# First expert layer's results stored in slot order and gathered by token in the attention stage, in a two-layer block on one Trainium2 core

## The reference

```python
# layer 0, experts: 8 experts, hidden size 512, two per token
h = layernorm(x) * (1 + cb) + sb
top_w, top_idx = top_k(softmax(h @ router_w.T), 2); top_w /= top_w.sum() + 1e-9
y = relu(h @ w1[e].T + b1[e]) @ w2[e].T + b2[e]          # for the token's two experts e
x = x + gb * (top_w[0] * y[0] + top_w[1] * y[1])
# layer 1, mixer ("attention")
h = layernorm(x) * (1 + ca) + sa
xn = h * rms_weight / sqrt(mean(h * h) + eps)
s  = gated_scan(sigmoid(xn @ w_A + b_A), (xn @ w_x) * sigmoid(xn @ w_output))
x  = x + ga * ((sigmoid(xn @ w_sidegate) * s) @ w_o + h)
# layer 1, experts: 16 experts, hidden size 256, two per token
```

## Time and profile before

| | us |
|---|---|
| time, median of 3 runs (lowest to highest) | 678.8 (677.65 to 682.81) |
| span of the profiled execution | 729.4 |
| time of the profiled execution around the span | not recorded |
| first to last tile of the first expert layer in the profile (first `up0` to last scatter) | 320.6 to 445.4 |
| attention, up to the first sigmoid, in the profile | 446.8 to 481.4 |

### The profile page before, as it was taken

One profiled execution on the slowest core, in us unless ns is written; L12 is line 12 of the kernel. 1 busy time (PEld: TensorE's weight loads), 2 busy tenths in 40 slices (PEclk: granted clock), 3 DMA queues, 4 the chain that ended last, 5 costly groups with the idle time before them and its releaser, 6 DMA issues.

```text
span 729.4 us, 9280 instructions
## 1 busy us (share of the span) xinstructions
PE 547.5 (75%) x2190; PEld 331.5 (45%) x2191; DVE 476.8 (65%) x847; ACT 340.9 (47%) x680; POOL 423.8 (58%) x324
## 2 busy tenths in 40 slices
PE   7599779989977889676676695669977677567730
PEld 3234224334423334555576683237545565446620
DVE  5867989997899898822532243646913777745427
ACT  3747445654755443412212235655615778950005
POOL 2576869998986897055555654500065771277650
PEclk8869969989997799978989998989968999796765
DMA  5432424332232330135556675000111121311115
GB/s 179 133 102 80 154 78 168 109 115 102 103 116 69 119 96 20 34 105 154 179 146 182 171 231 144 1 1 1 58 40 36 44 41 14 126 40 43 43 56 154
DMA packets 45438, 69.06 MB, mean 95 GB/s; under 512 B 6162, under 2 KB 25460, under 8 KB 45268
## 3 DMA queue, kind: packets, MB, share of 16 engines
q1 hardware_dynamic: 39828, 57.17, 25.1%
q0 software_dynamic: 5568, 11.41, 5.9%
HBM read 59.45 MB, written 9.11 MB: 94 GB/s over the span
## 4 chain that ended last, share of the span: by engine, by line
PE 53%; DVE 13%; issue 13%; ACT 9%; DMA 4%; another core or an unknown queue 3%; DVEq 2%; POOL 2%; SPq 1%; ACTq 1%; POOLq 0%
PE ps L1180 12%; PE ps L1325 6%; PE ps L1336 5%; PE ps L1143 4%; PE ps L1521 4%; DVE hs L1820 4%; PE ps L1174 4%; PE ps L1376 2%; PE ps L1485 2%; PE ps L1510 2%; PE ps L1087 1%; DVEq L1886 1%; DVE prod L1830 1%; ACT ps L709 1%
## 5 line engine op out<-in xcount | busy, mean ns | idle before, releaser
L521 POOL TENSOR_TENSOR bu<-uT,b_sb 128x1024 f32<-128x1024 f32 x62 | 145.0, 2356 | 1.6 <-DVE uT L1792 1.4
L475 POOL DMA_INDIRECT y_dram<-ys,rows_i x87 | 91.1, 1048 | 91.0 <-DVE ys L2078 38.2
L1180 PE MATMUL ps<-prod,cst 128*128 128x512 f32 x256 | 130.6, 655 | 3.2 <-DVE yT L1840 3.2
L469 POOL DMA_INDIRECT xl<-h_dram,rows_i x87 | 90.3, 1038 | 68.5 <-DVE rows_i L1704 36.1
L709 ACT ACTIVATE ps<-dtT,neg_a 128x512 f32<-128x512 f32 x128 | 85.5, 686 | 64.7 <-DVE hs L1820 63.6
L532 POOL TENSOR_TENSOR prod<-hs,c_sb 128x1024 f32<-128x1024 f32 x32 | 75.6, 2363 | 38.4 <-DVE hs L1820 21.4
L1180 PEld LDWEIGHTS ps<-prod,cst 128*128 128x128 f32 x256 | 50.4, 207 | 82.4 <-issue 77.1
L1820 DVE TENSOR_TENSOR_SCAN hs<-ps,carry,bu 128x512 f32<-128x512 f32 x64 | 77.6, 1264 | 4.5 <-ACT ps L709 4.5
L1820 DVE TENSOR_TENSOR_SCAN hs<-ps,bu 128x512 f32<-128x512 f32 x64 | 74.0, 1206 | 7.4 <-ACT ps L709 7.2
L1336 PE MATMUL ps<-w_s,ht 128*128 x312 | 47.5, 300 | 32.8 <-issue 19.4
L842 ACT ACTIVATE ht<-ps,b1T 128x128 f32<-128x128 f32 x78 | 24.7, 366 | 86.0 <-PE ps L1325 56.4
(11 more groups left out here) (293 smaller groups left out, 950.1 us busy)
## 6 DMA issues: line engine op xcount, KB each, us to landing
b_sb<-b_rows SPq DMA_DIRECT2D x31, 512.0 KB
w1r<-in_w SPq DMA_DIRECT2D x39, 256.0 KB
c_sb<-b_rows SPq DMA_DIRECT2D x32, 256.0 KB, 3.6
mf_s<-in_mf SPq DMA_DIRECT2D x16, 256.0 KB
w_s<-in_w SPq DMA_DIRECT2D x9, 256.0 KB, 4.0
h_dram<-h_tok SPq DMA_DIRECT2D x8, 256.0 KB
phase_s<-in_phase SPq DMA_DIRECT2D x16, 128.0 KB
down_s<-in_down SPq DMA_DIRECT2D x1, 2048.0 KB, 7.4
```

Source lines behind the costliest of these rows:

```text
L469: pool.indirect_dma_start(xl[:, j % slots, :], None, h_dram[l], bass.IndirectOffsetOnAxis(ap=rows_i[:, 0, j:j + 1], axis=0)).then_inc(load ...
L475: pool.indirect_dma_start(y_dram[l], bass.IndirectOffsetOnAxis(ap=rows_i[:, 1, j:j + 1], axis=0), ys[:, j % XR, :], None).then_inc(saved[j ...
L521: nc.gpsimd.tensor_tensor(bu[:, g % RING, :, :], uT[:, c % 2, :, :], b_sb[:, k % BRING, g % 2, :].unsqueeze(1).broadcast_to([P, ND, CHUNK] ...
L1180: last = nc.tensor.matmul(bank(Y_BANK + d), ident, prod[:, g % RING, d, :], start=n == 0, stop=n == NS - 1)
```

## The change

The first layer's results are stored as they come. `y_dram[0]` now has one row for each slot (39 * 128), and SP stores tile j of `ys0` to rows j * 128 and up with a plain DMA (`store_tile`), five tiles behind its weight loads; the second layer's weights stay where they were among the loads. `bias_down` waits for these stores in place of the scatters. POOL only gathers inputs during the layer, up to 16 tiles ahead. When all stores have landed, POOL gathers the results by token: for each of the 16 token tiles and both picks one indirect DMA that reads 128 rows of `y_dram[0]` by the slot numbers (`slot_i`, which VectorE copies out of `slot_f`), 32 in all, in the order of the chunks. SP's 8 loads are gone. What POOL did in the attention's entry moves: the weighting to ScalarE (4 instructions a chunk), the inverse deviation to ScalarE (`rstd`, two small instructions a chunk) and VectorE (`minus_mean`, one). VectorE's list of output rows for the first layer is no longer made. Some semaphores of early loads are merged.

```diff
+STORE_LAG = 5
+SR = 4
-AHEAD0 = 13
...
+            def store_tile(j):
+
+                if j >= SR:
+                    sp.wait_ge(stored[j % SR], 16 * (j // SR))
+                sp.wait_ge(S["dn_sb0"], j + 3)
+                sp.dma_start(y_dram[0][j * P:(j + 1) * P, :], ys0[:, j % XR, :]).then_inc(stored[j % SR], 16)
+
             sp.wait_ge(S["tiles_ready"], 1)
             for j in range(ST0):
...
+                if j >= STORE_LAG:
+                    store_tile(j - STORE_LAG)
+            for j in range(ST0 - STORE_LAG, ST0):
+                store_tile(j)
...
-            for c in range(NCHUNK):
-                load_rows(0, ST0, c, y0)
...
-            for j in range(AHEAD0):
+            for j in range(ST0):
                 take_rows(0, j, xl0, 2 * XR)
-            for j in range(ST0):
-                put_rows(0, j, ys0, j)
-                if j + AHEAD0 < ST0:
-                    take_rows(0, j + AHEAD0, xl0, 2 * XR)
...
+            def take_results(c):
+
+                for t in range(c * CT, (c + 1) * CT):
+                    for k in range(2):
+                        pool.indirect_dma_start(y0[k][:, t, :], None, y_dram[0],
+                                                bass.IndirectOffsetOnAxis(ap=slot_i[:, k, t:t + 1], axis=0)).then_inc(loaded[2 * c + k], 16)
+
+            pool.wait_ge(S["slots_ready"], 1)
+            for u in range(SR):
+                pool.wait_ge(stored[u], 16 * len(range(u, ST0, SR)))
+
+            for c in range(NCHUNK):
+                take_results(c)
...
+            def weigh_first(c):
+
+                for k in range(2):
+                    act.wait_ge(loaded[2 * c + k], results_in(2 * c + k))
+                for t in range(c * CT, (c + 1) * CT):
+                    ins = nc.scalar.activation(y0[0][:, t, :], y0[0][:, t, :], ACT.Copy, scale=wts[:, 0, t:t + 1])
+                ins.then_inc(S["y_scaled"], 1)
+
+            weigh_first(0)
+            rstd(2, 0)
             normed_in(0)
+            weigh_first(1)
             columns_in(0)
+            rms_columns(0)
+            rstd(2, 1)
             normed_in(1)
-            rms_columns(0)
+            weigh_first(2)
             columns_in(1)
+            rms_columns(1)
+            rstd(2, 2)
             normed_in(2)
-            rms_columns(1)
+            weigh_first(3)
             columns_in(2)
+            rms_columns(2)
+            rstd(2, 3)
             normed_in(3)
-            rms_columns(2)
             columns_in(3)
             rms_columns(3)
             act.preload_act_table_set(SIGMOID)
...
                 if j >= XR:
-                    dve.wait_ge(saved[j % XR], 16 * (j // XR))
+                    dve.wait_ge(stored[j % SR], 16 * ((j - XR) // SR + 1))
...
+            def minus_mean(c):
+
+                dve.wait_ge(S["ln_rstd"], 2 * NCHUNK + c + 1)
+                nc.vector.scalar_tensor_tensor(out=ln_nmr[:, c, :], in0=ln_mv[:, c, :, 0], scalar=-1.0, in1=ln_rs[:, c, :],
+                                               op0=ALU.mult, op1=ALU.mult).then_inc(S["rs1"], 1)
```

105 lines of the change are left out of this document (49 added, 56 removed).

## The result

| | kernel before | changed kernel |
|---|---|---|
| time, median (lowest to highest), us | 678.2 (671.8 to 682.8), 4 runs | 702.0 (694.4 to 707.2), 4 runs |
| span of the profiled execution | 729.4 | 692.6 (time 694.4) |

The ratio is 1.030, with a 95% interval from 1.022 to 1.038: the change costs about 20 us. Its time is 1.8 us above its span, and in every later execution the difference lies between 1.75 and 1.93 us. So a span of 729.4 us belongs to an execution of about 731 us. The experiments come back to that.

A forecast was written before the change was run, and what follows sets the result against it. Without late-news waits, POOL's gather and scatter pairs were taken to bound the first expert layer. Layer -2.7, stores 0, gathers +21.9, rest 0 gave +19.2 us on the 678.8 median: 698 us, range 685 to 714.

The forecast's parts named there:

- The span of 730 to 755: Whole kernel: expected span of the changed kernel's profiled execution, 730 to 755 us.
- The lower end of the layer: First expert layer: all tile steps at 1.87 us, a gain of 9.1 us; it gave the range's 689 us.
- the 50.6 us: Whole kernel: profiled span 729.4 less median 678.8 us, taken mainly as late-news waits absent from timed executions, 30.3 in the layer.
- The layer: First expert layer without scatters: paced by TensorE, ScalarE, VectorE and weight loads, ending at 413.8 against 416.5, a 2.7 us gain.
- POOL's pairs at 2.56 us: Old first expert layer: a gather and a scatter together take POOL 2.56 us, which bounds the layer.
- SP's 39 stores at nothing: First expert layer: stores queued among SP's weight loads cost 0, with 12.6 us as the other end.
- no wait of SP over 1 us for a result: First expert layer: a sign that the forecast is right, SP never waiting over 1 us for a tile's result.
- The 32 gathers, +21.9: Attention entry: POOL's gather issue plus a 14.7 us tail make 56.5 us to the first sigmoid against 34.6, plus 21.9.
- 56 us whatever the layer does: Attention entry in the profile: the reload's counterpart to the first sigmoid takes 56 us, however long the layer is.
- The late news is real and POOL's scatters cause it: First expert layer, rival: without scatters it gains 33.0 us, total 668 us; 7 in 100 (half of it, 684: 8).
- SP delays the weights: First expert layer, rival: each store pushes the next `w1` by its issue, +12.6 us, total 711; 8 in 100.
- Gathers slowed by VectorE: Attention entry, rival: gathers beside VectorE's work take 1.41 us, not 0.95; 14.3 us more, total 712; 6 in 100.

The follow-up runs named there:

- level A: The quicker of two states in which whole groups of runs stayed; the unchanged kernel before had medians of 678 and 675 us there.
- f1: The changed kernel run again with no edit, on level B: 748.1 us, ratio 1.036 to the kernel before.
- level B: The slower of two states in which whole groups of runs stayed; the unchanged kernel before had medians of 725, 724 and 723 us there.
- g1: f2 with two pauses put into POOL's 32 result gathers, on level A: 703.2 us, ratio 1.040 to the kernel before.
- g2: e2 with 32 unused memsets on POOL from the end of the layer, on level A: 681.2 us, ratio 1.012 to the kernel before.
- g3: e2 with 32 indirect gathers on POOL into a buffer nobody reads, on level A: 684.8 us, ratio 1.018 to the kernel before.
- f6: Kernel before with an unused memset on POOL ahead of each scatter, on level B: 722.6 us, ratio 0.997.
- f4: e2 with the attention entry of the kernel before (weighting and inverse deviation on POOL, old orders), on level B: 709.3 us, ratio 0.983 to the kernel before.
- e2: Changed kernel with 8 plain loads by SP in place of the 32 result gathers, on level B: 715.9 us, ratio 0.986 to the kernel before.
- f2: Changed kernel with POOL's input gathers held to six tiles ahead of TensorE, on level B: 735.4 us, ratio 1.019 to the kernel before.
- h1: Kernel before with 6 input gathers ahead of the first scatter in place of 13, on level B: 726.5 us, ratio 1.007.
- e3: Changed kernel with the layer's scatters kept and the 32 gathers added behind, on level B: 758.9 us, ratio 1.044 to the kernel before.

## Why the prediction was right, and where it wasn't

The time: 698 was predicted, 702.0 measured (or 698.3 by the ratio, 1.0296 x 678.2); the range of 685 to 714 holds it. The sign and the size were right on level A. The span of 730 to 755 that I expected for the profile was not: it is 692.6, a level A execution, and f1 on level B has 746.0. One sum was wrong. The lower end of the layer, a gain of 9.1, gives 678.8 - 9.1 + 21.9 = 692 us and not 689, as I took the 9.1 off a forecast that already held 2.7 of it. By its own steps:

**What the 50.6 us are: wrong.** The prediction put them down to waits that "are not in the timed executions". They are in the timed executions of level B, at which the profiled execution was taken, by its stretches. My reading of where they are was right in part: the stretches differ between the levels by about 31 to 34 us in the layer (131.1 and 133.9 against 99.4 to 100.5, of which the old layer's share on level A isn't seen) and by 14 to 19 behind the first sigmoid (246.2 to 249.8 against 231.1 to 232.5). But 315.7 - 303.8 = 11.9 us lie ahead of the first gather, where I looked for nothing, and have no late news in them. With 248.0 - 231.3 = 16.7 behind the sigmoid and an unchanged entry, some 22 to 24 us are left for the layer, an estimate, where I had 30.3. The sum was to stand against level A, so the error didn't reach the result. Against the kernel's own profiled level it would have: there the same sum was due at 722 to 725 plus 19, 744 us at the most, and the change took 748.1.

**The layer: right in size, the cause not shown.** Predicted for the change 413.8 - 315.74 = 98.1 us from the first gather, measured 100.5. From ScalarE's first to its last half tile it is 89.7 us against 77.4 + 9.4 = 86.8. The insertions of VectorE were costed at their length, 9.4 us. In the trace after the tile steps around them are 322.91 - 319.54 = 3.4 and 342.82 - 333.95 = 8.9 us, 12.3 less two steps of about 1.9, 8.5. From the last half tile to the first result gather it is 404.29 - 399.36 = 4.9 against 2.4 + 2.3 + 0.1 = 4.8. The gain over the old layer is worked out, not seen: the whole lost 20.1 us by the ratio, the entry 57.0 - 34.6 = 22.4, which leaves a gain of 2.3 for the rest. That is no proof of the 2.7 predicted: the interval of the ratio puts it between a gain of 7.6 and a loss of 3.0, and the same sum over g1, g2 and g3 gives a loss of 4.3, a gain of 0.5 and a loss of 3.8. The gain can't be told from nothing. That POOL's pairs at 2.56 us bound the old layer on level A stays an inference. On level B it is wrong, as f6 shows.

**SP's 39 stores at nothing: not shown, and not quite right.** The layer is near my pace, but loads of weights did come late. Where SP waits for nothing, its loop takes 2.05 us a tile with a store in it, where TensorE needs 1.90. TensorE stood idle 7 times, 5.7 us together, ahead of the product that needs the tile's `w1`:

```profile
PE ps L1341 <- issue: 5.7, 7, 1.6
...
361.55 1.13 PE L1341 MATMUL ps<-xt,w1r 128*128 128x128 f32 x8 [1.35 <-issue]
```

(The first line is of the waits from 309 to 400 us.) The view names no releaser, but the trace has the count of the load's semaphore 0.09 us ahead of each of the seven products, here at 361.46. The two profiles of the kernel before have 0.9 us of such waits and none. So at most 5.7 us of the 12.6 that I kept as the other end came. Whether the stores cause them or the faster layer does was not tested. One sign also failed, "no wait of SP over 1 us for a result". SP waited up to 4.0 us (waits of SP, 300 to 400 us: 7.6 us in 4 waits for VectorE's results) while VectorE did its inserted work; TensorE had nothing to miss from it at that time.

```profile
SPq L427 <- DVE ys L1926: 7.6, 4, 4.0
```

**The 32 gathers, +21.9: right as a sum, and on level A to 0.5 us** (57.0 us against 56.5). POOL's pitch is 1.27 against 1.25 us. The tail was costed at 14.7 behind the last landing, and the trace has 15.1 from the last weighting on. Inside it one term was wrong: I had the third chunk's columns and root, 4.0 us, ahead of the last chunk's work. In the trace they lie beside it. VectorE works on the last chunk from 447.44 to 451.36 while ScalarE does them, up to 451.38. I had left out the way through VectorE, 3.9 us, and that it is as long as the term it lies beside is luck. The last chunk's own columns and root took 5.0 us (455.00 to 459.98) against 4.0, and the weighting 1.3 against 1.65. Also missing was the cost of the new order itself, 6.8 us (f4 to e2), hidden in this kernel behind the 10 us a chunk. With it a chunk's work is 7.6 us and not "under 6", which is why ScalarE waits 1.7 to 2.6 us for each chunk and not "some 5". "56 us whatever the layer does" held on level A alone; on level B it is 74.2. The gathers alone therefore cost 13.9 us (g3 to the change) and the chain that they hide another 7 to 9. Taking only one of the two away brings less than 22 us: e2 without any gather still has an entry of 43.5 us.

**The rivals.** "The late news is real and POOL's scatters cause it" had its first half right on level B: the news is late in timed executions too, and without scatters the layer is 12.5 to 16.0 us shorter (f4, e2). But its conclusion, 668 us and faster, was wrong. Late news stands beside the long runs of gathers as well, and on level B the change is slower still, by 3.6%. What the layer wins there (about 13 us without any pause, 29 with those of f2, by the stretches) the entry loses (39.6 us, 74.2 against 34.6). "SP delays the weights" came in part at most, with the 5.7 us above. "Gathers slowed by VectorE" hardly came: 28 of the 32 took 0.94 or 0.95 us, the others at most 1.14, which is 0.02 us on the mean.

What stays open: what sets the level, whether it is POOL's issuing or the transfers that hold TensorE's news back, and by which path, and whether pauses in the result gathers (g1) bring the change level with the kernel before on level B. Behind the first sigmoid no experiment was made on the 14 to 19 us; the traces of level B have waits put down to "remote" there, 16.5 us in the profile before and 25.0 in f1 (summed over the engines), those of level A none. No version that gives the reference's result beat the kernel before. f4 and e2, which did on level B, load rows in slot order.

## What to carry to other kernels

Compare a profile's span with the times of its own execution before explaining a gap. Most of the 50 us between the two was, by the stretches, a difference of two levels, and 1.8 us the whole cost of what lies around the span. Here an indirect gather of 128 rows costs its engine 1.25 us whether or not the data is wanted, so 32 of them in place of 8 plain loads put 40 us ahead of the last consumer; count the chunk's issue time against the work on a chunk (10 us against 7.6 here), and only the larger of the two shows. Where news of TensorE is late while POOL issues one DMA behind the other, let POOL wait for the consumer: a pause cost the layer nothing on one level (100.3 us in g1) and shortened it by 15.7 us on the other, 12.7 us of the time (f2). The same idea in the kernel before, h1, won nothing.

## What the runs showed of the hardware that I had not expected

The same program has two levels, 675 and 723 us, that last through a group of runs. The granted clock is the lower one on the slower level (0.883 to 0.896 and 0.850 to 0.877 for the kernel before), but ahead of POOL's first indirect gather both time and clock are the same, so it isn't what sets them apart. On the slower one the end of a product on TensorE becomes known to ScalarE, VectorE and POOL up to 23.6 us late. No wait is put down to "remote" ahead of POOL's first indirect DMA in any trace. In four of the longest it came 2.0 to 3.6 us after POOL had ended an unbroken run of them:

| run | POOL's last issue ends | the waiting engine starts | its wait |
|---|---|---|---|
| f1, layer | 327.68 | 331.24 | 16.25 |
| f1, entry | 463.57 | 466.97 | 20.59 |
| f2, entry | 449.20 | 452.62 | 20.58 |
| e3, entry | 475.52 | 477.52 | 19.21 |

An unbroken run doesn't always hold the news back to its end. In e2 a late one came at 315.72 in the middle of one, 20 gathers from 301.28 to 326.18:

```profile
315.26 0.94 POOL L492 DMA_INDIRECT xl<-h_dram,rows_i  x1 [0.30 <-issue]
315.72 0.62 ACT L845 ACTIVATE ht<-ps,b1T 128x128 f32<-128x128 f32 x2 [7.74 <-remote]
316.50 0.95 POOL L492 DMA_INDIRECT xl<-h_dram,rows_i  x1 [0.30 <-issue]
```

On the faster level no wait of any engine is put down to "remote" in any of the four traces (after, g1, g2, g3), with the same unbroken runs of gathers. And a memset of 128x512 f32 took POOL 0.54 us, one of 128x1024 1.01 us (32.22 / 32).
